# A fused four-stage network block: the first layer norm taken tile by tile as the input arrives, with the weight products moved behind the first projections

## The reference

```python
def _ln_c(v, eps=1e-6):                      # over the 128 channels of a token
    return (v - mean(v)) / sqrt(var(v) + eps)

x = x + conv0(_ln_c(x))     # q, k, v = three projections; softmax over positions;
                            # out = einsum of global descriptors, then @ Wr + br
t = x.reshape(tokens)
t = t + moe(_ln_t(t))       # softmax gate, top 2 of 8 experts, gelu(t@W1[e]+b1[e])@W2[e]+b2[e]
x = x + grouped_conv3x3(_ln_c(t))
t = t + ode(_ln_t(x))       # a chain of RK4 steps from token 0 of each image, one per token:
                            # f(y) = tanh(tanh(y@W1.T+b1)@W2.T+b2)@W3.T+b3
```

## Time and profile before

| what | value |
|---|---|
| three timed runs | 2864.23, 2869.14, 2873.52 us (median 2869.14) |
| profiled execution, its own time | 2866.97 us |
| span from first to last instruction | 2864.7 us |
| mean granted TensorE clock | 0.985 of full speed |
| TensorE busy over the span | 98% |
| VectorE, ScalarE, GpSimd busy | 82%, 54%, 27% |

### The profile page before, as it was taken

The page is one execution under the profiler, slowest core; times in us unless marked ns, Lnnn a source line. Parts: engine busy times, 40 slices in busy tenths (PEclk is TensorE's granted clock), DMA queues, the critical chain, the costliest instruction groups (busy, mean ns, idle before and its releaser), DMA issues.

```text
span 2864.7 us, 207841 instructions
## 1 busy us (share of the span) xinstructions
PE 2798.6 (98%) x81958; PEld 2399.7 (84%) x81958; DVE 2348.9 (82%) x13248; ACT 1553.5 (54%) x10132; POOL 774.5 (27%) x1393
## 2 busy tenths in 40 slices
PE   8799999999999999999999999999999999999999
PEld 4578888888888888888888887888889999999998
DVE  5688888888888888888888887888878888888887
ACT  7555555555555555555554444444445555555555
POOL 5833233233233233323322000111122222222222
PEclk9789999999999999999999999999999999999999
DMA  3000000000000000000000000000000000000000
GB/s 119 3 14 11 11 15 11 11 15 11 11 14 12 11 11 15 11 11 15 11 11 9 0 0 1 0 0 0 0 17 0 0 0 0 0 0 0 0 0 15
DMA packets 21984, 28.24 MB, mean 10 GB/s; under 512 B 4384, under 2 KB 12896, under 8 KB 21544
## 3 DMA queue, kind: packets, MB, share of 16 engines
q1 hardware_dynamic: 21928, 27.48, 3.1%
HBM read 25.24 MB, written 2.23 MB: 10 GB/s over the span
## 4 chain that ended last, share of the span: by engine, by line
PE 93%; DVE 3%; ACT 2%; issue 1%; DMA 0%; SPq 0%; POOLq 0%; DVEq 0%; POOL 0%; ACTq 0%
PE PSUM L702 23%; PE PSUM L708 21%; PE PSUM L910 17%; PE PSUM L763 12%; PE PSUM L693 5%; PE PSUM L906 4%; DVE PSUM L1427 1%; PE PSUM L800 1%; PE PSUM L866 1%; PE PSUM L871 1%; PE PSUM L729 1%; ACT HA L1100 1%; PE PSUM L733 1%; PE PSUM L770 1%; PE PSUM L523 0%
## 5 line engine op out<-in xcount | busy, mean ns | idle before, releaser
L1427 DVE TENSOR_REDUCE PSUM<-PSUM 128x32 f32<-128x64 f32 x2912 | 624.8, 232 | 97.4 <-PE PSUM L708 51.9
L702 PEld LDWEIGHTS PSUM<-HA,RL 128*128 128x128 f16 x11648 | 396.2, 96 | 205.8 <-ACT HA L1100 194.7
L1101 ACT ACTIVATE PSUM<-PSUM 128x32 f32<-128x32 f32 x2912 | 561.2, 194 | 0.0
L1100 ACT ACTIVATE HA<-PSUM 128x32 f16<-128x32 f32 x1456 | 289.0, 199 | 472.1 <-DVE PSUM L1427 472.0
L1100 ACT ACTIVATE HB<-PSUM 128x32 f16<-128x32 f32 x1456 | 289.2, 200 | 465.6 <-DVE PSUM L1427 465.5
L702 PE MATMUL PSUM<-HA,RL 128*128 128x16 f16 x11648 | 511.9, 170 | 15.5 <-ACT HA L1100 7.6
L702 PE MATMUL PSUM<-HB,RLU 128*128 128x16 f16 x11648 | 511.4, 170 | 3.7
L435 POOL TENSOR_TENSOR G<-G 128x512 f16<-128x512 f32 x256 | 296.9, 1160 | 683.1 <-ACT G L1073 683.1
L708 PE MATMUL PSUM<-HA,RH 128*128 128x32 f16 x11648 | 465.7, 177 | 0.0
L708 PE MATMUL PSUM<-HB,RHU 128*128 128x32 f16 x11648 | 464.4, 177 | 0.0
L702 PEld LDWEIGHTS PSUM<-HB,RLU 128*128 128x128 f16 x11648 | 393.8, 96 | 46.9 <-ACT HB L1100 2.0
(11 more groups left out here) (315 smaller groups left out, 6726.8 us busy)
## 6 DMA issues: line engine op xcount, KB each, us to landing
G<-scores SPq DMA_DIRECT2D x64, 256.0 KB, 3.1
N<-in_x SPq DMA_DIRECT2D x8, 256.0 KB, 4.7
NHL<-in_w SPq DMA_DIRECT2D x1, 2048.0 KB, 9.9
STF<-in_w SPq DMA_DIRECT2D x1, 2048.0 KB, 14.5
out<-W2HL SPq DMA_DIRECT2D x8, 256.0 KB, 2.4
G<-in_r SPq DMA_DIRECT2D x1, 1024.0 KB, 5.1
R1K<-in_r SPq DMA_DIRECT2D x1, 256.0 KB, 2.7
R3F<-in_r SPq DMA_DIRECT2D x1, 256.0 KB, 5.3
```

Of the source, the lines that this page charges most:

```text
L702: mm(out[m // 2][:, 2 * B * (m % 2):2 * B * (m % 2) + B], lo[:, k, m], src[:, k, 0], start=False, stop=False)
L1100: A(hi[:, 2 * h:2 * h + 2, 0], src, ACT.Tanh, scale=1.0 / scale).then_inc(rk_hi, 1)
L1101: A(full, src, ACT.Tanh, scale=1.0 / scale).then_inc(rk_f, 1)
L1427: v.tensor_reduce(bank[:, SUM:SUM + 2 * B].rearrange("p (m b) -> p m b", m=2), bank[:, 0:4 * B].rearrange("p (m c b) -> p m b c", m=2, c=2 ...
```

## The change

Four things change, all ahead of the first attention round.

- TensorE's list: instead of 8 tiles of transposes and then the norm, a loop of 11 turns. Turn n holds the transposes of tile n, M of tile n-1, V of tile n-3.
- The copy out of the transposes' bank goes from ScalarE to VectorE, and VectorE's list becomes a loop of 12 turns: copy of tile n (called C below), D of tile n-2, N of tile n-4. ScalarE's list of S, L, E stays.
- Sums of the first norm use banks 2 to 7 in turn instead of bank t, and M of tiles 6 and 7 waits for the logarithm that last read that bank. The norm no longer waits for the small constants.
- The four weight products come behind `project(0)`.

```diff
-            for t in range(NT):
+            def turn_in(t):
                 pe.wait_ge(x_in[t], 16)
                 if t >= 2:
                     pe.wait_ge(x_c, t - 1)
 ...
-            layer_norm(0, fuse)
+            for n in range(NT + 3):
+                if n < NT:
+                    turn_in(n)
+                t = n - 1
+                if 0 <= t < NT:
+                    if t == 0:
+                        pe.wait_ge(consts, 1)
+                    if t >= 6:
+                        pe.wait_ge(ln_log, t - 5)
+                    pe.wait_ge(x_c, t + 1)
+                    mm(PS[2 + t % 6][:, :], ONES[:, :], X[:, bass.ts(t, TILE)], start=True, stop=True).then_inc(ln_mean, 1)
+                t = n - 3
+                if t >= 0:
+                    pe.wait_ge(ln_sq, t + 1)
+                    mm(PS[2 + t % 6][:, :], ONES[:, :], SQ4[:, t % 4], start=True, stop=True).then_inc(ln_var, 1)
 ...
             project(0)
+            pe.wait_ge(rk_in, 16 * len(ODE))
+            for k in range(MC):
+                mm(PS[k][:, :], R3N[:, bass.ts(k, 128)], R1K[:, :], start=True, stop=True).then_inc(rk_13, 1)
 ...
-            with act.Fori(0, PAIRS) as i:
-                for par in range(2):
-                    act.wait_ge(x_tr, 2 * i + par + 1)
-                    nc.scalar.copy(X[:, tile(i, par)], PA[par][:, :]).then_inc(x_c, 1)
 ...
+            for n in range(NT + 4):
+                if n < NT:
+                    dve.wait_ge(x_tr, n + 1)
+                    v.tensor_copy(X[:, bass.ts(n, TILE)], PA[n % 2][:, :]).then_inc(x_c, 1)
+                t = n - 2
+                if 0 <= t < NT:
+                    if t >= 4:
+                        dve.wait_ge(ln_out, t - 3)
+                    dve.wait_ge(ln_mean, t + 1)
+                    TT(D4[:, t % 4], X[:, bass.ts(t, TILE)], PS[2 + t % 6][:, :], ALU.subtract).then_inc(ln_dev, 1)
+                t = n - 4
+                if t >= 0:
+                    dve.wait_ge(ln_sd, t + 1)
+                    TT(N[:, bass.ts(t, TILE)], D4[:, t % 4], SQ4[:, t % 4], ALU.mult).then_inc(ln_out, 1)
```

More of the change, by code:

```diff
@@ L958, in layer_norm @@
                         act.wait_ge(ln_var, NT * p + t + 1)
-                        A(SQ4[:, t % 4], PS[t][:, :], ACT.Ln, bias=EPS[:, eps:eps + 1]).then_inc(ln_log, 1)
+                        A(SQ4[:, t % 4], PS[t if p else 2 + t % 6][:, :], ACT.Ln, bias=EPS[:, eps:eps + 1]).then_inc(ln_log, 1)
                     t = n - 2
@@ L965, in _ @@
             nc.scalar.preload_act_table_set("natural_log_exp_and_others")
-            with act.Fori(0, PAIRS) as i:
-                for par in range(2):
-                    act.wait_ge(x_tr, 2 * i + par + 1)
-                    nc.scalar.copy(X[:, tile(i, par)], PA[par][:, :]).then_inc(x_c, 1)
             act.wait_ge(consts, 1)
+            layer_norm(0, 0)
             act.wait_ge(w_in, 16 * len(SMALL))
-            layer_norm(0, 0)
             def copy_kq(i):
@@ L1177, in _ @@
             v.memset(ONES[:, :], 1.0 / C).then_inc(consts, 1)
+            for n in range(NT + 4):
[12 more added lines that the diff above has]
+                    TT(N[:, bass.ts(t, TILE)], D4[:, t % 4], SQ4[:, t % 4], ALU.mult).then_inc(ln_out, 1)
+            dve.wait_ge(ln_out, NT)
             dve.wait_ge(w_in, 16 * len(SMALL))
-            layer_norm(0)
             def maxima(i, which):
```

## The result

The changed kernel takes 2876.78 us (median of 12 runs, 2871.93 to 2879.33), the kernel before 2869.43 on the same chip: ratio 1.0026, 95% interval 1.0017 to 1.0035. Measured a second time, beside other kernels, it was 2877.39 against 2863.84: 1.0051 (1.0038 to 1.0065). The two differ mostly in the kernel before, whose runs stand in two groups (more on that in the experiments). It is a small loss, near the bound of 0.3%; the forecast was 2874.6. The profiled execution of after took 2877.36, 10.4 more than that of before.

What follows compares the result with a forecast made beforehand. TensorE was busy nearly throughout, so opening delays reach the end. Shift 4.4 at the mark plus 1.6 for the clock is 6.0, less 0.5 is +5.5: 2866.97 becomes 2872.5, plus 2.2 gives 2874.6; range 2866 to 2882.

Steps and rivals of the forecast that it cites:

- The early start: First norm no longer waits for all tiles: N of tile 0 at 15.1, 5.0 ahead of before.
- The ring: First norm: closed loop D, S, L, E, N, C, D on VectorE and ScalarE; 4.01 a tile, 3.39 without copy, against 1.72.
- The rival: First norm: loop doesn't close, TensorE sets the pace; last variance at 24.1, `project(0)` at 24.9, time 2863.9; chance 8%.
- `project(0)`: First projection after the norm: starts at 34.6, 4.6 later than before; early start gained 5.0, ring lost 9.6.
- The products: Four weight products behind `project(0)`: 3.44 on the path, partly covered by the old 2.73 pause and slow 3.52.
- The clock in the ring: First norm, 26.8 to 34.6: sparse TensorE work makes the clock fall; 1.6 taken, between nothing and 8.1.
- the mark: End of the opening, first copy of transposed exponentials: 42.48 before, forecast 46.9 (4.4 later) without the clock term.
- The rival with the low clock through the products: Clock stays low from the last variance through the weight products: 12.0 later, time 2881; chance 13%.
- What comes behind: After the opening: GpSimd keeps its times, later readers wait for nothing more; 0.5 comes back, between nothing and 1.
- the forecast's base: Whole kernel before: profiled execution of 2866.97, with the median of the runs 2.2 above it.

Runs made afterwards that it cites:

- the opened ring: Changed kernel with N one turn later on VectorE, behind the deviation three tiles ahead instead of two: 2865.95 us, 0.9997 of the kernel before.
- the ring filled: Changed kernel with the variance products of tiles 3 to 6 done three times over: 2874.20 us against 2877.39 of the changed kernel, 1.0042 of the kernel before.
- The filler in round 3: Changed kernel with the key product of the last attention round's own tiles done again, unread: 2873.25 us, 1.0020 of before; also tried in other kernels.
- the products alone: Kernel before with only the four weight products moved from between the variances to behind `project(0)`: ratio 1.0005; its profiled run took 2863.74 us.
- the three others: Profiles of the products alone (1.0005), the changed kernel with products back between the last variances (1.0017), and the opened ring with VectorE copying W13 (0.9994).

## Why the prediction was right, and where it was not

**The early start** was sized nearly right: N of tile 0 at 15.79, forecast 15.1. TensorE's work ahead of it ends at 12.69 where I had 11.75, mostly for the first mean, which took 2.05 instead of 0.86; the links from there to N are 0.25 shorter than I had them.

**The ring** is what I said it was, in its order and its members. Its length is 3.68 and 3.08, forecast 4.01 and 3.39: each link was 0.01 to 0.12 shorter (D to S 0.72 against 0.81, N to the next 0.61 against 0.73). The copy was forecast at 0.62 and costs 0.60 from start to start. It runs for 0.69 and the deviation for 0.68, both with a source in PSUM; the lower end, 0.41 with its source in SBUF, was not reached. The experiment that opened the ring shows that without it `project(0)` would start at 26.7. The rival had said 24.9, with TensorE setting the pace throughout; but the first mean was slow there too (2.04), and the last tiles went at the pace of ScalarE's three steps, so that the last variance began at 24.73.

**`project(0)`** came at 34.81, forecast 34.6, by two errors that cancel. N of tile 5 was 0.9 early (32.99 against 33.9). But `project(0)` waited last for the logarithm of tile 7 (34.03 to 34.72), which I had done by then; the last variance, which that logarithm reads, ran at half clock, 2.08 instead of about 1.1. With the ring filled it starts at 33.26, 0.6 of it from the earlier first N.

**The products** cost 3.63 on the path, forecast 3.44. Their net cost is small because of the pause that they replace, as I said. In the kernel before they even gain 0.8.

**The clock in the ring** is the term that was mis-sized. I had its place (between 26.8 and 34.6; measured 29.4 to 39.6) and wrote 1.6, "what the nearest fall cost": 3.52 less 1.92 for the first half of `project(1)`, under the low clock of 36.2 to 39.6. It costs 3.3 at the mark. The old fall lay across half a projection; this one lay across the last variance (2.08 against 1.12), all of `project(0)`'s first half (3.75 against 1.95) and part of the second (2.41 against 1.86), and these three add up to the 3.3. What this fall cost is the work that lay under it, and I took over the price of another fall instead of adding that work up. The rival with the low clock through the products was half right: low until 39.6, but the products themselves ran at full speed (3.63, behind 40.97). What is left of the 7.3 at the mark, 4.0, is the ring and the products at full clock, forecast 4.4; the sum was 6.0.

**What comes behind** is the step that failed. I wrote that GpSimd's list hides nothing and that about 0.5 comes back. GpSimd hid nothing indeed, and of the 13.4 by which the second norm's first variance was late (82.17 to 95.58) 12.75 are left at the first tanh, which no run ties to my reason for the 0.5. But 4.0 were added in round 3 by a fall of the clock, and 2.1 in the means behind it. Nothing in the profile of before shows the fall, for there the round ran at 1.00; what it does show is a TensorE that is busy for only 3.53 of 5 us at 70 to 75. I looked for later stages that could absorb the shift, and not for one that stood near a fall of the clock. The filler in round 3 shows the cause: with it the round runs at 1.00 (in the trace of after with it, from 38.4 to 86.2), and of the 4.0 it gives back 3.0, its own work counted in. What makes one execution of the same round fall and another not, I can't say from these runs; the opened ring, 3.2 early, fell as well. It happened in every profile without the filler but that of before: for 17.1 us in both of after and in the opened ring, 13.7 with the ring filled, and 3.4 in the three others, one of which, the products alone, differs from before by 0.8 at the mark. So I can't say that the shift brought the fall about.

The three times that set the forecast's base hid this too: before has runs with and without what I take to be the same fall, and its median moves between 2863.84 and 2869.43 with the share of each. The forecast of the time, 2.2 below the first measurement, is better than its terms, and that is in part luck: the base, 2869.14, came from the upper group, and so did the median of before in that measurement (2869.43), where the shift between the medians is 7.35. In the second measurement the shift is 13.55, and between the two profiles 10.4, which is 4.9 above my 5.5.

Open: the shift falls from 12.75 to 10.4 on the way to the end. About 0.7 goes in the first RK4 steps, of which fewer lie in the low clock (159.93 to 172.8 against 147.18 to 162.5); the rest was not followed. The first tanh also has a scatter of its own: with the products alone it stands at 144.13, 3.05 earlier than before, though the second norm there begins 0.42 later (79.05); between the two the clock is low for 33 us in that profile and for 43 in that of before.

## What to carry to other kernels

Where two in-order engines pass a tile to and fro, write the links down in the order of both lists: if each engine's next step waits for the other's last one, the loop's length is the pace, whatever the busy shares say, and one more place between the two uses opens it (3.68 to 2.15 here). The stretch that left TensorE idle here was priced by the work behind it that then ran slow, 3.3 us in the ring, and 2 us of products that nobody reads were worth 3 in round 3, their own time counted in. A sparse stage that kept its clock in one profile can lose it in the next, so look at the stages behind a change for TensorE's idle time too, and take more than one profile where the times stand in two groups.

## What the hardware showed

The clock column says 1.00 from the first instruction, but the first products run at about half the later rate. TensorE's start in the kernel after, in order of time:

```profile
6.11 2.05 PE L556 MATMUL PSUM<-X,ONES 128*128 128x512 f32 x2
...
10.16 1.02 PE L556 MATMUL PSUM<-X,ONES 128*128 128x512 f32 x2
```

The same sum takes 2.05 at 6.11 and 1.02 at 10.16; four transposes take 0.85 at 8.16 and 0.44 at 9.88. The clock's own record in this trace begins at 8.9 us, with full speed, and so does that of before. So the column is not to be trusted before the first record, and the 1.00 in the first line of the earlier trace rows had spoken against a slow start without ground.

The clock stayed low here while TensorE was busy again: in round 3 of after it was busy for 5.00 of 5 us at 80 to 85 and for 4.15 at 85 to 90, at 0.50 all along, and the clock rose at 94.3.
